# Two feed-forward passes around a power-ReLU attention: a new order of the product ring, and the projection of batch 0 inside it

## The reference

```
x = x + 0.5 * ffn(layernorm(x))
x = x + attention(layernorm(x))
x = x + 0.5 * ffn(layernorm(x))        # same weights as the first
```

## Time and profile before

| | us |
|---|---|
| median of 3 runs (477.25 to 478.65) | 478.63 |
| the profiled execution | 477.65 |
| its span, first to last instruction | 475.9 |
| PE / DVE / ACT / POOL busy | 409.9 / 396.4 / 323.8 / 281.0 |

### The profile page before, as it was taken

One profiled execution on the slowest core, in us unless ns is written; L12 is line 12 of the kernel. 1 busy time (PEld: TensorE's weight loads), 2 busy tenths in 40 slices (PEclk: granted clock), 3 DMA queues, 4 the chain that ended last, 5 costly groups with the idle time before them and its releaser, 6 DMA issues. The chain is left out here.

```text
span 475.9 us, 13631 instructions
## 1 busy us (share of the span) xinstructions
PE 409.9 (86%) x5040; PEld 192.3 (40%) x5040; DVE 396.4 (83%) x928; ACT 323.8 (68%) x584; POOL 281.0 (59%) x205
## 2 busy tenths in 40 slices
PE   0779999761889999999999999999999875889996
PEld 0323444341244444444444444444444453334442
DVE  5886555886899999999999999999999988675443
ACT  3323222554799999999999999999999704422221
POOL 5960000044689999999999999999999800000000
PEclk9989999987899999999999999999999998899999
DMA  4300000005661504205105032051003100000001
GB/s 117 89 1 0 1 0 0 1 26 106 212 122 40 81 9 78 48 4 100 25 26 87 15 70 55 3 101 25 3 6 80 41 11 0 2 0 22 0 22 44
DMA packets 18140, 19.92 MB, mean 42 GB/s; under 512 B 4808, under 2 KB 10536, under 8 KB 18088
## 3 DMA queue, kind: packets, MB, share of 16 engines
q1 hardware_dynamic: 17736, 19.11, 18.9%
q10 hardware_dynamic: 352, 0.07, 0.1%
HBM read 13.02 MB, written 6.03 MB: 40 GB/s over the span
## 5 line engine op out<-in xcount | busy, mean ns | idle before, releaser
L1249 POOL TENSOR_TENSOR arena<-arena 128x1024 f32<-128x1024 f32 (+1 forms) x144 | 240.7, 1704 | 20.3 <-ACT arena L1221 19.6
L1182 DVE SCALAR_TENSOR_TENSOR arena<-bank,masks 128x512 f32<-128x512 f32 x288 | 179.9, 681 | 8.2 <-PE bank L1088 8.2
L1221 ACT ACTIVATE arena<-arena 128x1024 f32<-128x1024 f32 (+1 forms) x160 | 147.9, 959 | 1.1 <-DVE arena L1182 0.2
L1088 PE MATMUL bank<-Q,K 128*32 128x512 bf16 (+3 forms) x1536 | 96.5, 331 | 23.4 <-DMA K<-k_parts 10.3
L1211 ACT ACTIVATE bank<-bank 128x1024 f32<-128x1024 f32 (+5 forms) x144 | 90.0, 625 | 8.0 <-PE bank L1088 7.4
L1088 PE MATMUL bank<-K,Q 128*32 128x512 bf16 (+3 forms) x1536 | 93.0, 329 | 0.0
L1188 DVE TENSOR_SCALAR_CACHE_REDUCE bank<-bank 128x896 f32<-128x896 f32 (+4 forms) x112 | 83.9, 778 | 0.0
L1125 PE MATMUL bank<-arena,Vq 128*32 128x512 f32 (+3 forms) x768 | 77.0, 486 | 0.0
L624 ACT ACTIVATE arena<-bank 128x512 f32<-128x512 f32 x40 | 23.9, 597 | 75.3 <-PE bank L499 75.3
L1088 PEld LDWEIGHTS bank<-Q,K 128*32 128x32 bf16 x1536 | 37.2, 96 | 89.5 <-issue 22.5
L725 DVE TENSOR_TENSOR arena<-arena,bank 128x512 f32<-128x512 f32 x40 | 27.4, 685 | 41.7 <-PE bank L503 41.6
(11 more groups left out here) (122 smaller groups left out, 349.1 us busy)
## 6 DMA issues: line engine op xcount, KB each, us to landing
Q<-q_parts SPq DMA_DIRECT2D x24, 192.0 KB
K<-k_parts SPq DMA_DIRECT2D x16, 128.0 KB
att<-arena SPq DMA_DIRECT2D x28, 64.0 KB, 1.6
K<-k_parts SPq DMA_DIRECT2D x8, 192.0 KB
X<-in_L_attn_x SPq DMA_DIRECT2D x4, 256.0 KB, 4.3
K<-k_parts SPq DMA_DIRECT2D x16, 64.0 KB
out_x<-X SPq DMA_DIRECT2D x4, 256.0 KB, 2.3
q_parts<-arena SPq DMA_DIRECT2D x3, 256.0 KB
```

Source lines behind the costliest of these rows:

```text
L1088: last = nc.tensor.matmul(m.bank[j:j + 32, at + lo:at + hi], left[par][:, g, blk * P + j:blk * P + j + 32], right[par][:, g, s0:s0 + hi - ...
L1182: nc.vector.scalar_tensor_tensor(Y(r, g)[:, y0:y0 + SPAN], m.bank[:, at:at + SPAN], 0.0, mask, ALU.max, ALU.mult).then_inc(relu_done, 1)
L1221: nc.scalar.activation(z, Y(r, g)[:, tile_low(r) - off(r):T - off(r)], ACT.Square)\
L1249: nc.gpsimd.tensor_tensor(z, z, z, ALU.mult).then_inc(fourth_p, 1)
```

## The change

1. *Start.* The load block becomes `Start` and runs inside f1's block. The weights are issued directly behind x. f1's norm is done per span (four parts). POOL's `attention_constants` wait until all routing weights are ready (`parts_ready` 2).
2. *Ring.* gate and up of a chunk are an "item". A span's order is now shared chunk first, then the 4 routed ones (`ORDER`). 5 items are issued ahead of the first down (`AHEAD`); further ones are handed out by `issued_by`, spread evenly over the 20 steps, so that the lead shrinks to nothing. A step n is: spread (routed steps), the new items, turn_back of the span before (shared steps), down. `hid` has 6 buffers. The loop is written out. The same code runs f2, with 20 items and no projection.
3. *Projection.* `project_qkv` is gone; `Project` puts batch 0's q and k (items 20 and 21) and v (item 22) behind f1's 20 items in the ring, with norm, transposes and splits at fixed steps; batch 1's follow in the same block. SP stores whole batches of 128 rows and loads quad 0 when the six stores of batch 0 are done. Batch 1 is stored in attention's block.
4. *Bias.* POOL's addition of `bp` to X goes; in `Merge` PE puts it into the projection's PSUM bank by a matmul with the identity ahead of the projection.

```
 def load_weights(...):
+    # order now: sw_gate, sw_up (shared_loaded), w_gate, w_up (experts_loaded), sw_down, w_down (down_loaded), then attention's
...
+AHEAD, NHID = 5, 6
+ORDER = [NCH, 0, 1, 2, 3]
...
+    items = [("ffn", n) for n in range(LAST)]
+    if project is not None:
+        items += [("qk", 0), ("qk", 1), ("v", 0)]
+    in_steps = len(items)
+    if project is not None:
+        items += [("qk", 2), ("qk", 3), ("v", 1)]
+    def issued_by(n):
+        return AHEAD if n < 0 else min(in_steps, AHEAD + -(-(n + 1) * (in_steps - AHEAD) // (LAST - 1)))
+    def new_items(n):
+        return range(issued_by(n - 1), issued_by(n))
+    ROOT, TILES, TURN, HIGH_Q, CENTRE, HIGH_K, MIDDLE_Q, REST_K, NORM2 = 12, 12, 14, 16, 17, 18, 19, 19, 17
...
+            def item(r):                                   # PE
+                if r >= 2:
+                    pe.wait_ge(silu_ready, r - 1)
+                ...                                        # gate, q rows or 4 v tiles -> gate_ps[r % 2]
+                if r >= 2:
+                    pe.wait_ge(prod_ready, r - 1)
+                ...                                        # up, k rows or 4 v tiles -> up_ps[r % 2]
...
             logits(0)
+            item(0)
             for i in HALVES[1]:
                 norm_transpose(nc, m, s, pe, i)
             turn_scores(0)
+            item(1)
             logits(1)
-            products(0, 0, False)
+            item(2)
             turn_scores(1)
-            products(0, 1, False)
+            for r in range(3, AHEAD):
+                item(r)
             pe.wait_ge(parts_ready, 1)
             turn_weights(0)
+            for n in range(LAST):
+                if n == HCH: ...                           # wait parts_ready 2, turn_weights(1..3)
+                if project is not None and n == TURN: ...  # project.transpose(0)
+                if routed(n):
+                    spread(n)
+                for r in new_items(n):
+                    item(r)
+                if n and not routed(n):
+                    turn_back(span_of(n) - 1)
+                down(n)
+                if project is not None and n == TURN: ...  # project.transpose(1)
+            if project is not None:
+                project.transpose(pe, 2, xt_ps[2])
+                turn_back(NSPAN - 1)
+                item(in_steps)
+                project.transpose(pe, 3, xt_ps[3])
+                item(in_steps + 1)
+                item(in_steps + 2)
...
+            # ACT, step n: take_out of the span before, (ROOT) Sqrt table and two roots, the new items' SiLU or
+            # q_full or v copy, last tiles, takes, (16) high q, (NORM2) Sqrt table and root 2, (18) high k, (19) middle q
             take_out(NSPAN - 1)
+            project.take(act, 2, xt_ps[2])
+            item(in_steps)
+            act.wait_ge(project.norm.moments_ready, 4)
+            norm_root(nc, m, project.norm, act, 3)
+            project.middle_part(act, "k", 0)
...
+            # POOL behind attention_constants
+            project.rest_part(pool, minus, "q", 0)
+            project.v_full(minus, 0, project.v_raw)
+            project.low_part(pool, minus, "q", 0)
+            project.low_part(pool, minus, "k", 0)
...
+            # DVE: routing of span 0 with items between
             scores(0)
             pick_groups(now)
+            item(0)
             pick_experts(now)
+            item(1)
             scores(1)
             weigh(now)
+            for r in range(2, AHEAD):
+                item(r)
+            for n in range(LAST):
+                if routed(n):
+                    scale(n)
+                ...                                        # n = 0, 1, 2: pick_groups, pick_experts, weigh (later)
+                for r in new_items(n):
+                    item(r)
+                if place_of(n) == 1 and n > 1:
+                    add_to_x(span_of(n) - 1)               # f1: with statistics and moments
+                ...                                        # 12, 13: norm_vector 0, 1; 17: centre_k, norm_vector 2; 19: rest k
...
+    def store_and_load(self, sp):
+        self.store(sp, 0)
+        sp.wait_ge(self.m.parts_stored, 16 * 2 * PARTS)
+        sp.wait_ge(self.m.operands_zeroed, 4)
+        load_quad(self.nc, self.m, sp, self.dram["q"], self.dram["k"], 0, 0)
...
     def tensor(self, pe, sums, sums_out, last_sums):       # Merge
+                for k in range(TPS):
+                    nc.tensor.matmul(self.proj_ps[i][:, k * P:(k + 1) * P], m.ident[:, :], m.bp[:, :],
+                                     start=(k == 0), stop=True, skip_group_check=True)
                 pe.wait_ge(self.att_ready, i + 1)
...
-                                            m.WP[:, :], start=True, stop=True)
+                                            m.WP[:, :], start=False, stop=True, skip_group_check=True)
```

More of the change, by code:

```diff
@@ L247, in load_weights @@
     sp.wait_ge(m.attention_loaded, 16 * ATTENTION_DMAS)
[L250 to L295, removed]
@@ L384, in norm_vector, with norm_tiles @@
         .then_inc(s.rstd_ready, 1)
-    for t in range(t.start, t.stop):
+def norm_tiles(nc, m, s, dve, first, last):
+    for t in range(first, last):
         if t % TPS < TPS - 1:
@@ L629, in _ @@
-            span(0, True)
-            for j in range(1, NSPAN):
-                take_weights(j)
-            with act.Fori(1, NSPAN) as i:
-                span(i, False)
-            if following is not None:
-                nc.scalar.activation(m.table[:, :], m.eps[:, :], ACT.Sqrt)
-                act.wait_ge(following.moments_ready, 1)
-                norm_root(nc, m, following, act, 0)
-            take_out(NSPAN)
-            if following is not None:
-                for i in range(NSPAN // B):
-                    norm_last_tile(nc, m, following, act, i)
-                for i in range(NSPAN // B):
-                    norm_take(nc, m, following, act, i)
@@ L646, in _ @@
+        if start is not None:
             @block.sync
             def _(sp):
+                start.sync(sp)
                 load(sp)
+                project.store_and_load(sp)
         if out is not None:
@@ L745, in span @@
-            def span(i, first):
-                for c in range(HCH):
-                    h = hid[:, HID[c], :]
-                    if not (first and c == 0):
-                        product(i, c)
-                    if c < NCH:
-                        dve.wait_ge(prod_ready, i * HCH + c + 1)
-                        dve.wait_ge(spread_ready, i * NCH + c + 1)
-                        nc.vector.tensor_tensor(h, h, spread_ps[c % 2], ALU.mult).then_inc(hid_ready, 1)
-                    if first and c == 0:
-                        pick_groups(later)
-                    if first and c == 1:
-                        pick_experts(later)
-                    if first and c == 2:
-                        weigh(later)
-                    if c == 2 and not first:
-                        add_to_x(i)
@@ L763, in _ @@
-            span(0, True)
-            with dve.Fori(1, NSPAN) as i:
-                span(i, False)
-            if following is not None:
-                for n in range(NSPAN // B):
-                    last = span_moments(nc, m, dve, n, stats_ready)
-                last.then_inc(following.moments_ready, 1)
-                for n in range(NSPAN // B, NSPAN - 1):
-                    span_moments(nc, m, dve, n, stats_ready)
-                norm_vector(nc, m, following, dve, 0)
-            add_to_x(NSPAN)
```

660 lines of the change are left out of this document (392 added, 268 removed).

## The result

The changed kernel takes 482.5 us (median of 4 runs, 482.04 to 483.48); the kernel before took 478.28 beside it (4 runs, 477.25 to 478.65). The ratio is 1.0094, 95% interval 1.0071 to 1.0118: slower by 0.9%, clear of the noise. The forecast was 482.0. The profiled execution took 482.41, its span is 480.6, 4.7 longer than before.

What follows compares the result with a forecast made beforehand. PE bounds the passes inside, DVE their beginnings, a chain the hand-over to attention. 477.65 − 1.8 (front) + 5.8 (second pass) + 0 = 481.65, plus 0.35 gives 482.0; range 477.2 to 485.8.

Steps and rivals of the forecast that it cites:

- the 0.35 added at the end of the sum: Added to the 481.65 sum because the median lies 1.0 above the profiled run, giving 482.0.
- Second pass: Second feed-forward pass: routing queued behind item 0 and steps without an item make the last down later, 5.8 us lost.
- Start and early first pass: First pass's beginning: norm done at 13.7 instead of 20.5, span 0's weights at 30.6 instead of 28.7, PE 6.0 ahead.
- Projection in the ring: First pass's steps with projection work and waits added: last down at 96.75 instead of 87.9.
- Tail: Last down to attention: low k at 103.65, store 3.3, load 10.8; attention begins at 117.8 instead of 119.6, 1.8 gained.
- Bias on PE: Merge: 16 bias matmuls, 0.9 to 1.0 per span, fit into PE's waits: 0; without that cover 3.8.
- In the difference already: Front: removing POOL's 4.5 us bias addition and the 3.25 us DVE stall is already counted in the replaced chain's difference.
- (1): Rival: attention starts with the projection block's end at 113.5, not quad 0's load; 6.1 gained, 477.4; chance 0.14.
- (2): Rival: the lead pays in both passes; second pass's last down 3 earlier than now, 473 in all; chance 0.10.
- (3): Rival: port contention blocks the tail; the 3.25 stall returns at the k centring, step 17: 485; chance 0.11.
- (4): Rival: projection does not fit the ring; batch 0's q and k reach PE before its xnT: 484; chance 0.11.
- The rule on the port: Two-SBUF-input DVE instructions contend with POOL instructions reading SBUF, not with ones only writing; memsets beside the ring cost nothing.

Runs made afterwards that it cites:

- the routing first: Changed kernel; in the second pass the second logits go ahead of items on PE, span 0's routing ahead of products on DVE: 479.15 us, ratio 1.0012.
- The two small edits of the front: Kernel before, with projection bias moved from POOL to PE in the merge and POOL's attention constants made after the first pass's routing: 470.27 us, ratio 0.9825.
- the routing first (43.09): Changed kernel with old second pass, batch 0's middle k early, and first-pass second logits and span 0 routing ahead of items and products: 472.15 us, ratio 0.9855.

## Why the prediction was right

The sign and the mechanism came out as worked, and the time within 0.5: 5.60 lost for 5.8 in the second pass, and in the front 0.95 gained for 1.8 (0.6 to 1.9 by the other profiles of this front). That the numbers fit so closely is in part luck: inside both terms errors of 1 and more nearly cancel, and the 0.35 added at the end of the sum has no row behind it. Point by point:

*Second pass.* Right in mechanism, and shown by the runs: the old pass gives all of it back, the routing first 3.35. The forecast wait of PE for SiLU 0 was 2.7, it is 2.60; the idle time of DVE 3.8, it is 3.92. Four of the five steps without an item start their down 1.23 after their spread, the very price of the forecast (the bracket says 0.85, as it counts from the recorded end of the spread, 0.16 behind its pitch of 0.22); at step 18 it is 1.58. Step 5 waits 0.68 for 0.6. The forecast times are those of a pass whose first logits start at 401.69; here they start 0.94 sooner, so times are compared from there. Item 0 at half clock was wrong: it ended after 4.23 for 5.3, as the clock rose sooner than in the earlier trace rows, the weights were ready after 16.37 for 17.7, and step 4 ended after 33.08 for 34.2, 1.1 sooner than forecast. What follows took 41.97 for 41.0: 0.35 more at step 18, and the downs behind waits, which take about 0.1 more than the 0.86 of the others (447.77 to 448.74, 461.35 to 462.31). The two errors nearly cancel.

*Start and early first pass.* The norm ended at 13.61 for 13.7. The weights came at 28.66 for 30.6, again because item 0 ran at full clock; the fall of the clock after the 2.60 wait, which gave back some of that, I had not foreseen. Step 4's down ended at 46.4 for 47.8, step 5's at 50.8 for 51.9.

*Projection in the ring.* The waits were where I put them: steps 7 and 12 0.48 each for 0.9, step 13 1.04 for 1.4, step 17 0.49 for 1.0, step 18 3.13 for 2.7, step 19 0.85 for 1.0. Step 10's down ended near 65.7 for 66.95, the last at 97.2 for 96.75. Steps 11 to 19 took 31.5 for 29.8, although their waits in brackets were together 1.0 shorter than mine: what failed is first the full clock that I gave them. Behind the 3.13 wait steps 18 and 19 ran at 1.2 GHz, some 1.6 more by their pitches (0.35 at the one down, 0.25 at the spread, 1.0 at the other). Of the other 1.1 some 0.8 is in how a wait is read: at steps 12, 13 and 17 the bracket leaves out 0.16, and the down behind it takes 0.96 or 0.97 instead of 0.86. Waits too long and PE too fast nearly cancel at the ring's end.

*Tail.* The right order of events, and the right late-comer: ACT's middle k stands behind the fourth root, low k ends at 104.74 for 103.65, the loads begin 2.86 later for 3.3 and take 11.07 for 10.8. "Batch 1's splits end about 113.0, with the barrier 113.5" was mis-sized: the V sum on POOL ends at 116.71. I had not seen that the k centring of batch 1 would stand 2.58 instead of 0.75 beside POOL's subtraction, 1.83 of the 3.7; the rest I have not placed. It did not count here, as the load was later still; in the run with the middle k early it became the bound at once.

*Bias on PE.* Nothing, as forecast. Timeline of PE in the merge of the changed kernel:

```profile
389.90 1.99 PE L1433 MATMUL bank<-den,spread 128*128 128x256 f32 x8 [0.88 <-DVE den L1492]
```

The additions stand in the waits: that of 2.67 for the second reciprocal has become 0.88.

*What the net sum of the front hid.* "In the difference already" was true and taught too little. The two small edits of the front give 7.91 in the old orders (119.62 to 111.71), and the changed kernel has the same two and shows 0.95. So the rest of the change (start, orders, ring) costs 7.0 net in the front: 2.1 for the middle k's place, until the block's end takes over (118.67 to 116.56), 2.5 for the early items (to 114.05), and 2.3 that is left to the ring and its tail by subtraction alone (to 111.71); no run isolated that last part. Profiles of one and the same front differ by up to 1.3 (117.71 to 118.98), so the three sizes are rough, and the middle one has the clock in it. I had argued that early items put PE "6.0 ahead". Against the kernel before they do: its fifth down ends at 46.86, here it ends at 46.46 with four items more, 7.3 ahead. But most of that is the earlier norm's: with the two small edits alone the fifth down ends at 41.58, so the new front is 2.0 ahead of that, and 5.4 with the routing first (43.09).

*The rivals.* (1) The block's end did not decide in this profile, since the load again took 11; POOL's V sum ended 2 before it. In the run with the old second pass, on the same front, the block's end did decide, and it does in the runs with the loads earlier: the two are closer than the forecast's 4.3. (2) The lead did not pay in the second pass; in the first it was worth 2.0 at the fifth down, as said, and 5.4 with the routing first. (3) The port: one-column centring beside POOL's V sum took 1.11, not 3.25, the V sum not quite over; the rival in small. (4) The projection did fit the ring: PE waited for none of its inputs.

*The rule on the port.* The one-column sum, both of whose inputs lie in SBUF, took 3.25 beside POOL's addition and 0.16 alone. In the kernel before, the routing's tensor_tensor operations, also with both inputs in SBUF, took 0.16 to 0.21 beside POOL's memsets (23.5 to 24.7), about as with POOL idle in the changed kernel (0.16 to 0.20). Both agree with what the prediction cited. The scaling that keeps 0.69 beside the memsets reads one input from PSUM, so it does not test that rule. The norm tiles show more: 10.39 beside memsets that only write, 3.16 without. The Trainium skill (SBUF — State Buffer, Who interferes with whom) has a second rule for it: a tensor_scalar can run in a mode of DVE that uses the ports shared with GpSimd, and then one of the two waits for the other. The two rows agree with it, and so does the centring with 2.58 beside POOL and 0.75 alone.

## What to carry to other kernels

Before an order of a whole pass is changed, its small edits are to be run alone: here two of a few lines gave 1.7% together, and the reordering around them took all of that and more. Work that fills a wait is worth only what the chain behind the wait does not lose: put the head of a long chain of small operations (routing) ahead of products in each engine's queue, and use the products as filling behind it. Where an engine's order is written by hand, the instruction that a DMA waits for must not stand behind one that waits for something later.

## What was not expected of the hardware

The granted clock of PE fell to 0.50 behind waits of 2.13 to 3.13 us, but not every time. The kernel with the old second pass has the same first pass and the same wait of 2.60 at 23.44, and there these are its stretches:

```profile
24.00:26.00 2.00, 2.00 (x9) 0.91 (x8) 1.93 (x17) 0.60 (x1) 0.00 (x0) 1.00 0.00 0
26.00:28.00 2.00, 2.00 (x5) 0.71 (x5) 1.79 (x9) 0.60 (x1) 0.00 (x0) 1.00 0.00 0
```

The changed kernel has 0.72 and 0.50 there. Its first down starts at 33.09, that kernel's at 32.60, and the 0.49 stays until the down of step 18 (92.54 to 92.05). That down and the spread behind it run at full clock in that kernel, and the last down is 1.09 apart (95.33 to 94.24). So the clock alone moves this front by about 1, as much as the gain that the first subtraction gave. Whether the two groups of times in the run with the middle k early come from it stays open. The load of quad 0, 1.15 MB, took 10.5 to 11.1 us in every kernel in which PE waited for it.
